# Norms before cross attention and before the router: rows transposed without gain and shift, which ScalarE adds on the transposed rows and GpSimd on the kept rows later

## The chip, the cores and the metric

One Trainium2 chip, one NeuronCore. The time is the device time of one execution in microseconds (us). Below, PE is TensorE, PEld its weight loads, DVE is VectorE, ACT is ScalarE, Pool is GpSimd and SP is SyncE, whose queue issues most of the transfers. Each engine works through its own instructions in the order of the program; semaphores tie the engines together.

## The reference

Eight sequences ("lanes" in the kernel) of 256 rows with 256 columns go through two layers. Cut to what matters:

```python
# layer 0: norm first
x = x + attn(ln(x, ln1), ln(x, ln1), causal=True)        # call 0
x = x + attn(ln(x, ln2), ctx, causal=False)              # call 1
x = x + ffn(ln(x, ln3))
# layer 1: norm after
x = ln(x + attn(x, x, causal=True), ln1_g, ln1_b)        # call 2; its norm is "stage 3"
x = ln(x + attn(x, ctx, causal=False), ln2_g, ln2_b)     # call 3; its norm is "stage FINAL"
x = ln(x + moe(x), ln3_g, ln3_b)                         # router: top 2 of 8 experts
# ln(x, g, b) = (x - mean) / sqrt(var + eps) * g + b ; attn has 16 heads of 16 columns
```

The two norms in question are the one that feeds call 3 (stage 3) and the one that feeds the router and the experts (stage FINAL). Both results are used twice: transposed, as the input of a projection, and as kept rows `x[lane]`, which go on as the residual (stage 3) or to the experts (FINAL). The inputs give every gain and shift values other than 1 and 0.

## The kernel before

There are 32 attention calls (4 calls of the model x 8 lanes), started one after the other in slots. A call lives for several slots: norm, transpose, q/k/v projections, a first pass of scores for the row maxima (`"max"`), a second pass of scores with the exponentials (`"head"`), weighing, output projection. Parts of neighbouring calls are interleaved on every engine. The order is written in a table: `STEPS` lists each step with a time (`AT[...]`, in units of which 16 make a slot), and each engine sorts its own steps by that time plus its entry in `LAG[engine]`. These numbers fix only an order in each queue; nothing else is done with them.

In `"head"`, PE writes the scores of a head into one of two PSUM buffers (`s_0`, `s_1`, line 766), and ACT turns them into `probs` (line 985). PE can't write the next head but one before ACT has read the buffer. So an ACT instruction that waits, or that stands ahead of an exponential, can stop PE.

The norm for a lane of stage 3, and of FINAL for lanes 0 to 6 (`by_three`), has four parts. DVE makes mean and variance (`norm`, steps "ln"). Pool makes `rstd` and `offset` (`inverse_root`, lines 561 to 568). ACT applies both to the kept rows in place (`scale`, line 896, two instructions). Pool multiplies by the gain and adds the shift (`gain_and_shift`, lines 575 and 577), and raises `gained`. PE (`rows_T` for stage 3, `final_T` for FINAL, both line 669) waits for `gained`, through `wait_norm`, and transposes the rows; ACT copies the transposed rows out of PSUM (lines 884 and 901). For FINAL the router's product (line 826), the choice of experts on DVE, `rank` on PE, and Pool's `scatter` (line 635, four indirect transfers a lane) follow, and SP stores the rows (`store`, line 521). Lane 7's FINAL norm is made on DVE alone (`apply_norm`: lines 1035 and 1040) after Pool's `rstd` (line 570), since nothing else is left to run beside it.

For the norms of layer 0 (stages 0, 1 and FFN) the transposed rows already get gain and shift on ACT (line 882), since there the kept rows don't need them.

Where PE has nothing left to interleave (lanes 5 to 7 of FINAL), the kernel has it transpose a constant (line 650, `s<-ident`). At the end of this part all engines meet, and the experts' part begins: its first instruction on the SP queue is the load of line 1316.

## Time and profile before

| | |
|---|---|
| median of 3 runs | 1204.1 us (1203.78 to 1204.68) |
| profiled execution: own time | 1205.83 us |
| its span, first to last instruction | 1204.1 us |
| PE busy | 1077.1 us, 89% |
| DVE, ACT, Pool busy | 846.2, 760.2, 518.6 us |
| mean granted TensorE clock | 0.957 |

The execution's own time is its span and 1.7 us around it; it is 0.14% above the median of the runs. In the granted clock, 1.00 is 2.4 GHz and 0.50 is 1.2 GHz. In the timeline a row gives start, duration, engine, line, operation and shapes, with xcount where like instructions are merged (the duration is then that of the whole group), and in brackets for how long the engine sat idle before it and what it waited for.

### The profile page before, as it was taken

The numbers are of one execution on the slowest core, as the hardware profiler recorded it, in microseconds if no ns is written. First come the engines' busy times: TensorE is split into PE (matmuls) and PEld (weight loads), VectorE is DVE, ScalarE is ACT, GpSimd is POOL, SyncE is SP. The second block draws the span as 40 slices with busy tenths as digits, with TensorE's granted clock in tenths as the row PEclk, the third lists the DMA queues.
The fourth block names the chain that finished last, engine by engine and source line by source line (L and its number), as shares of the span: only waits on it lengthen the run. The fifth ranks groups of instructions, "written<-read, shape, count | busy, mean of one in ns | idle before, by whom it ended". The sixth has DMA issues, their size and how long they took to land. (4 is left out here: it accounts for less than half of the span.)

```text
span 1204.1 us, 27676 instructions
## 1 busy us (share of the span) xinstructions
PE 1077.1 (89%) x9213; PEld 893.6 (74%) x9213; DVE 846.2 (70%) x2539; ACT 760.2 (63%) x1587; POOL 518.6 (43%) x736
## 2 busy tenths in 40 slices
PE   7788889999999999998899988878889999999960
PEld 6466666778888888876667666655679999999960
DVE  2677888777766666657777677763367988888846
ACT  4355565667666666645566666545258988898832
POOL 4345556322222223445566346532433454454544
PEclk9699999999999999999999999988889999999985
DMA  7584656654344433445566566622547787877764
GB/s 172 95 177 77 92 84 112 93 92 65 53 63 63 71 54 54 77 55 82 79 140 111 106 126 107 96 54 91 198 146 210 233 244 224 236 236 234 247 167 147
DMA packets 110892, 152.40 MB, mean 127 GB/s; under 512 B 23104, under 2 KB 95296, under 8 KB 104384
## 3 DMA queue, kind: packets, MB, share of 16 engines
q1 hardware_dynamic: 100560, 138.64, 51.8%
q0 software_dynamic: 8352, 10.80, 4.6%
q10 hardware_dynamic: 1872, 1.60, 1.1%
q8 instruction: 58, 0.95, 0.4%
q14 instruction: 50, 0.41, 0.2%
HBM read 78.39 MB, written 21.62 MB: 83 GB/s over the span
## 5 line engine op out<-in xcount | busy, mean ns | idle before, releaser
L985 ACT ACTIVATE probs<-s 128x384 f32<-128x384 f32 (+1 forms) x512 | 263.7, 541 | 130.3 <-PE s L766 117.1
L1069 DVE TENSOR_REDUCE neg_max<-s 128x2 f32<-128x512 f32 x256 | 167.9, 688 | 70.5 <-PE s L741 63.9
L766 PE MATMUL s<-q_stack,k_stack 98*128 98x256 bf16 (+1 forms) x1024 | 176.9, 263 | 16.4 <-ACT probs L985 14.0
L624 POOL TENSOR_SCALAR_AFFINE_SELECT probs<-probs 128x256 f32<-128x256 f32 x256 | 103.9, 417 | 176.6 <-ACT probs L985 172.6
L1066 DVE CUSTOM_DVE_ANT_0 s<-s,mask_qk 128x256 f32<-128x256 f32 x256 | 114.7, 448 | 66.2 <-PE s L738 58.4
L766 PEld LDWEIGHTS s<-q_stack,k_stack 98*128 98x128 bf16 x1024 | 87.9, 99 | 47.8 <-ACT probs L985 35.2
L785 PE MATMUL pv<-probs,v 128*32 128x256 f32 (+1 forms) x2048 | 116.0, 369 | 4.7 <-POOL probs L624 4.7
L741 PE MATMUL s<-k_stack,q_stack 96*128 96x256 bf16 x512 | 96.0, 276 | 13.3 <-DVE neg_max L1069 11.9
L1456 PE MATMUL moe<-rows_hi,e_w_hi 128*128 128x256 f32 x368 | 103.8, 282 | 2.6 <-DVE rows_lo L1574 2.6
L1456 PE MATMUL moe<-e_w_hi,e_hidden_hi 128*128 128x256 f32 x368 | 104.6, 284 | 0.0
L1456 PE MATMUL moe<-rows_hi,e_w_lo 128*128 128x256 f32 x368 | 103.2, 280 | 0.0
L1456 PE MATMUL moe<-rows_lo,e_w_hi 128*128 128x256 f32 x368 | 103.1, 280 | 0.0
L687 PE MATMUL work<-hT,w_qk 128*128 128x256 f32 x384 | 95.0, 392 | 8.8 <-ACTq L886 8.1
L1456 PE MATMUL moe<-e_w_lo,e_hidden_hi 128*128 128x256 f32 x368 | 102.9, 279 | 0.0
L1456 PE MATMUL moe<-e_w_hi,e_hidden_lo 128*128 128x256 f32 x368 | 102.7, 279 | 0.0
L1578 DVE TENSOR_TENSOR e_hidden_lo<-e_hidden,e_hidden_hi 128x512 fp32r<-128x512 f32 x92 | 77.0, 837 | 35.2 <-ACT e_hidden_hi L1538 27.8
L785 PEld LDWEIGHTS pv<-probs,v 128*32 128x32 f32 x2048 | 62.4, 113 | 46.5 <-issue 22.4
L1404 POOL DMA_INDIRECT x_rows<-result,token x46 | 80.0, 1738 | 25.2 <-issue 25.2
L737 PE MATMUL s<-k_stack,q_stack 96*128 96x256 bf16 x256 | 69.6, 283 | 21.2 <-DVE neg_max L1067 17.7
L687 PEld LDWEIGHTS work<-hT,w_qk 128*128 128x128 f32 x384 | 70.8, 194 | 20.3 <-ACTq L886 9.0
L1067 DVE CUSTOM_DVE_ANT_0 s<-s,mask_qk 128x128 f32<-128x128 f32 x256 | 84.9, 332 | 0.0
L1396 POOL TENSOR_TENSOR result<-result,share 128x512 f32<-128x512 f32 x23 | 30.6, 1329 | 118.7 <-issue 96.4
(207 smaller groups left out, 2895.0 us busy)
## 6 DMA issues: line engine op xcount, KB each, us to landing
w<-in_expert_w SPq DMA_DIRECT2D x26, 1024.0 KB, 5.3
k_stack<-k_part SPq DMA_DIRECT2D x192, 128.0 KB, 4.0
q_stack<-q_part SPq DMA_DIRECT2D x180, 128.0 KB
w_next<-in_expert_w SPq DMA_DIRECT2D x22, 1024.0 KB, 5.2
rows<-slots_x SPq DMA_DIRECT2D x25, 256.0 KB
slots_x<-filler SPq DMA_DIRECT2D x8, 518.0 KB
cT<-in_context SPq DMA_DIRECT2D x16, 256.0 KB, 5.9
e_b<-in_expert_b SPq DMA_DIRECT2D x24, 128.0 KB
```

Source lines behind the costliest of these rows:

```text
L624: pool.affine_select(out=blocks, in_=blocks, compare_op=ALU.is_ge, fill=0.0, base=0, pattern=[[0, TILES], [1, P]], channel_multiplier=-1). ...
L687: last = pe.matmul(dst[:, half * S:(half + 1) * S], w[:, k, half * P:(half + 1) * P], src[:, k, :], start=(k == 0), stop=(k == KC - 1))
L741: last = pe.matmul(dst[:, qt * S:(qt + 1) * S], q[:, qt * P:(qt + 1) * P], k, start=True, stop=True)
L766: last = pe.matmul(dst[:, kt * S:kt * S + S - q0], k[:, kt * P:(kt + 1) * P], q[:, q0:S], start=True, stop=True)
L785: last = pe.matmul(pv[32 * j:32 * j + 32, g * S + q0:(g + 1) * S], v[n % 3][:, (kt * H + hd) * VW:(kt * H + hd) * VW + 2 * DK], probs_of(n ...
L985: act.activation(probs_of(n, hd)[:, 0:width], s2[hd % 2][:, 0:width], ACT.Exp, scale=SCALE).then_inc(probs_ready, 1)
L1066: dve.tensor_tensor_reduce(src[:, 0:S], src[:, 0:S], mask_qk[:].rearrange("p b s -> p (b s)"), -1.0, -MASKED, ALU.add, ALU.min, neg_max[:, ...
L1067: dve.tensor_tensor_reduce(src[:, S:S + P], src[:, S:S + P], mask_qk[:, 1, :], -1.0, -MASKED, ALU.add, ALU.min, neg_max[:, 0, hd:hd + 1]). ...
L1069: dve.tensor_reduce(neg_max[:, :, hd], src[:].rearrange("p (t s) -> p t s", t=TILES), AX_X, ALU.max, negate=True).then_inc(s1_free, 1)
L1404: pool.indirect_dma_start(x_rows, bass.IndirectOffsetOnAxis(ap=token[i][:, m:m + 1], axis=0), result[i][:, m, :], None, compute_op=ALU.add ...
L1456: last = pe.matmul(dst, lhs[a], rhs[b], start=first and m == 0, stop=end and m == 2)
L1578: dve.tensor_tensor(hidden_lo[i][:, 2 * q:2 * q + 2, :], hidden[:, 2 * q:2 * q + 2, :], hidden_hi[i][:, 2 * q:2 * q + 2, :].bitcast(F32), ...
```

## The change

Stage 3: `rows_T` now waits only for ACT's `scale`; ACT multiplies by the gain and adds the shift while it copies the transposed rows (line 884 becomes the form of line 882). The kept rows get the gain in `add_bias` on Pool, after the transposes; the shift is added once to the output bias row, so that it comes with the bias.

FINAL: `final_T` waits only for `scale` (lanes 0 to 6) or DVE's apply (lane 7, now two instructions and not four). ACT's copy of line 901 becomes two instructions with gain and shift. Pool's `gain_and_shift` comes after the transposes, now for all eight lanes; `store` and `scatter` wait for it.

In the table ACT's "scale" goes later by 0.7, "final_T" earlier by 0.8, and "gain" from 59.3 to 62.5 (plus Pool's lag of 2.8, unchanged). "gain" is no longer a step of stage 3.

```diff
-LAG = {"scalar": {... "out": 1.4, "scale": 2.5, "halve": 0},
+LAG = {"scalar": {... "out": 1.4, "scale": 3.2, "halve": 0},
-      ... "final_ln": 59.3, "final_T": 64.8, "store": 63.1,
+      ... "final_ln": 59.3, "final_T": 64.0, "gain": 62.5, "store": 63.1,
...
-    return [(at, kind, lane, stage) for kind in (("ln", "scale", "gain") if by_three(lane, stage) else ("ln", "apply"))]
+    return [(at, kind, lane, stage) for kind in (("ln", "scale") if by_three(lane, stage) else ("ln", "apply"))]
...
         def wait_norm(engine, lane, stage):
             if by_three(lane, stage):
-                engine.wait_ge(gained, nth("gain", lane, stage))
+                engine.wait_ge(scaled, nth("scale", lane, stage))
...
             def store(lane, _):
-                wait_norm(sp, lane, FINAL)
+                sp.wait_ge(gained, nth("gain", lane, FINAL))
...
             def gain_and_shift(lane, stage):
-                pool.wait_ge(scaled, nth("scale", lane, stage))
+                pool.wait_ge(work_full, filled("final_T", lane, stage))
...
             def add_bias(lane, stage):
+                if lane == 0 and stage in POST:
+                    pool.tensor_tensor(bo[stage], bo[stage], shift[stage], ALU.add)
+                    pool.drain()
                 pool.wait_ge(work_full, filled("T", lane, stage))
+                if stage in POST:
+                    pool.tensor_tensor(x[lane], x[lane], gain[stage].unsqueeze(1).to_broadcast([P, TILES, D]), ALU.mult)
+                    pool.drain()
                 pool.tensor_tensor(x[lane], x[lane], bo[stage].unsqueeze(1).to_broadcast([P, TILES, D]), ALU.add).then_inc(x_biased, 1)
...
             def scatter(lane, stage):
+                pool.wait_ge(gained, nth("gain", lane, stage))
...
             def final_T(lane, stage):
                 act.wait_ge(work_full, filled("final_T", lane, stage))
-                act.activation(hT_of[FINAL][:].rearrange("p k s -> p (k s)"), bank("final_T", lane, stage)[:], ACT.Copy).then_inc(final_T_ready, 1)
+                for k in range(KC):
+                    last = act.activation(hT_of[FINAL][:, k, :], bank("final_T", lane, stage)[:, k * S:(k + 1) * S], ACT.Identity, bias=shift_column[stage][:, k:k + 1], scale=gain_column[stage][:, k:k + 1])
+                last.then_inc(final_T_ready, 1)
...
             def apply_norm(lane, stage):
-                if stage in POST:
-                    for i in range(TILES):
-                        dve.scalar_tensor_tensor(out=x[lane][:, i, :], in0=x[lane][:, i, :], scalar=mean_var[k][:, i, 0:1], in1=gain[stage], op0=ALU.subtract, op1=ALU.mult)
-                    dve.drain()
                 dve.wait_ge(rstd_ready, nth("ln", lane, stage))
```

How the queues change. On PE, around FINAL's transposes of lane 4 (`s_0` and `s_1` are the score buffers; line 741 is the pass for the maxima, line 766 the pass for the exponentials, 669 the transposes, 826 the router). Before:

```order
L766 MATMUL s_1<-q_stack,k_stack 128x256 x2
L741 MATMUL s_0<-k_stack,q_stack 128x256 x2
L741 MATMUL s_1<-k_stack,q_stack 128x256 x2
L766 MATMUL s_0<-q_stack,k_stack 128x256 x2
L741 MATMUL s_0<-k_stack,q_stack 128x256 x2
L766 MATMUL s_1<-q_stack,k_stack 128x256 x2
L669 MATMUL work<-ident,x 128x128 x4
L766 MATMUL s_0<-q_stack,k_stack 128x256 x2
L741 MATMUL s_1<-k_stack,q_stack 128x256 x2
L826 MATMUL work<-router_w,hT_ffn_final 128x8 x4
```

The same place after the change (the lines are 7 higher):

```order
L773 MATMUL s_1<-q_stack,k_stack 128x256 x2
L748 MATMUL s_0<-k_stack,q_stack 128x256 x2
L748 MATMUL s_1<-k_stack,q_stack 128x256 x2
L773 MATMUL s_0<-q_stack,k_stack 128x256 x2
L676 MATMUL work<-ident,x 128x128 x4
L748 MATMUL s_0<-k_stack,q_stack 128x256 x2
L773 MATMUL s_1<-q_stack,k_stack 128x256 x2
L773 MATMUL s_0<-q_stack,k_stack 128x256 x2
L748 MATMUL s_1<-k_stack,q_stack 128x256 x2
L833 MATMUL work<-router_w,hT_ffn_final 128x8 x4
```

The transposes stand one maximum pass and one head earlier. In lanes 0 to 3 they also move ahead of the q projection (line 687), which stands between those two.

On ACT, the same lane: the copy `u<-pv` of the weighed values, the norm's `scale` (`x<-x,offset_final`), the exponentials, and the copy of the transposed rows. Before:

```order
L949 ACTIVATE u<-pv 128x512
L896 ACTIVATE x<-x,offset_final,rstd_final 128x256 x2
L985 ACTIVATE probs<-s_0 128x512
L985 ACTIVATE probs<-s_1 128x512
L985 ACTIVATE probs<-s_0 128x512
L901 ACTIVATE hT_ffn_final<-work 128x512
```

After:

```order
L958 ACTIVATE u<-pv 128x512
L994 ACTIVATE probs<-s_0 128x512
L903 ACTIVATE x<-x,offset_final,rstd_final 128x256 x2
L994 ACTIVATE probs<-s_1 128x512
L994 ACTIVATE probs<-s_0 128x512
L909 ACTIVATE hT_ffn_final<-work,columns 128x256 x2
```

One exponential has moved ahead of `scale`, and two still stand between `scale` and the copy, which is now two instructions.

On Pool, the end of its queue in this part, after the change (lane 6's gain, shift and lane 5's scatter come first, then lane 7's `rstd`, gain and shift, and then the scatters of lanes 6 and 7 together):

```order
L575 TENSOR_TENSOR x<-x,row 128x2x256
L577 TENSOR_TENSOR x<-x,row 128x2x256
L642 DMA slots_x<-x,slot_of 33024x259 x4
L561 TENSOR_TENSOR var_eps_final<-mean_var_final,eps 128x2
L570 TENSOR_TENSOR rstd_final<-var_eps_final,minus_half 128x2
L575 TENSOR_TENSOR x<-x,row 128x2x256
L577 TENSOR_TENSOR x<-x,row 128x2x256
L642 DMA slots_x<-x,slot_of 33024x259 x8
```

Before, the fifth row was followed directly by the eight indirect transfers; the two operations of lines 575 and 577 are new there.

## Rows read from the trace of the kernel before

**Rows 1.** Page, part 2: granted TensorE clock in 40 equal slices, in tenths.

```profile
PEclk9699999999999999999999999988889999999985
```

**Rows 2.** Windows: start:end, length, busy us (count) of PE, PEld, DVE, ACT, POOL, clock.

```profile
713.00:739.00 26.00, 23.27 (x201) 16.78 (x200) 19.43 (x56) 16.94 (x37) 15.99 (x21) 1.00 0.60 103
786.57:812.57 26.00, 19.97 (x157) 12.51 (x156) 15.17 (x45) 11.72 (x25) 8.75 (x11) 0.77 0.10 33
```

**Rows 3.** Waits of PE from 687 to 792 (FINAL, lanes 0 to 3): total, times, longest.

```profile
PE s L766 <- ACT probs L985: 4.0, 9, 0.8
PE work L826 <- ACT hT_ffn_final L901: 1.2, 4, 0.3
```

**Rows 4.** Waits of PE from 786 to 870 (FINAL, lanes 4 to 7).

```profile
PE s L766 <- ACT probs L985: 6.7, 7, 2.1
PE work L669 <- POOL x L577: 3.7, 3, 1.3
```

**Rows 5.** Timeline of lane 4, PE, ACT and POOL.

```profile
792.48 1.09 ACT L896 ACTIVATE x<-x,offset_final,rstd_final 128x256 f32<-128x256 f32 x2 [0.47 <-POOL offset_final L568]
793.48 1.06 ACT L985 ACTIVATE probs<-s 128x512 f32<-128x512 f32 x2
...
794.11 0.61 PE L766 MATMUL s<-q_stack,k_stack 98*128 98x256 bf16 x2 [1.69 <-ACT probs L985]
...
796.61 1.11 PE L669 MATMUL work<-ident,x 128*128 128x128 f32 x4 [1.04 <-POOL x L577]
...
798.41 1.87 PE L826 MATMUL work<-router_w,hT_ffn_final 128*128 128x8 f32 x8
```

**Rows 6.** Timeline of lanes 5 and 6: scale and router of each.

```profile
821.43 1.09 ACT L896 ACTIVATE x<-x,offset_final,rstd_final 128x256 f32<-128x256 f32 x2 [0.48 <-POOL offset_final L568]
...
827.06 1.87 PE L826 MATMUL work<-router_w,hT_ffn_final 128*128 128x8 f32 x8
...
845.98 1.09 ACT L896 ACTIVATE x<-x,offset_final,rstd_final 128x256 f32<-128x256 f32 x2
...
851.59 1.87 PE L826 MATMUL work<-router_w,hT_ffn_final 128*128 128x8 f32 x8 [0.69 <-ACT hT_ffn_final L901]
```

**Rows 7.** Timeline of lane 2: FINAL's transposes.

```profile
745.31 0.60 PE L669 MATMUL work<-ident,x 128*128 128x128 f32 x4
```

**Rows 8.** Timeline in layer 0: DVE beside Pool, and ACT's copy with gain and shift.

```profile
260.66 0.74 DVE L1042 TENSOR_SCALAR h<-x,mean_var_main,rstd_main 128x256 f32<-128x256 f32 x2 [0.19 <-issue]
...
261.60 1.18 POOL L607 TENSOR_TENSOR x<-x,row 128x512 f32<-128x512 f32 x1
...
261.73 1.52 DVE L1042 TENSOR_SCALAR o<-x,mean_var_ffn,rstd_ffn 128x256 f32<-128x256 f32 x2 [0.34 <-POOL rstd_ffn L570]
...
264.01 1.02 ACT L882 ACTIVATE hT_ffn_final<-work,columns 128x256 f32<-128x256 f32 x2
```

**Rows 9.** Windows before the fall of the clock, and behind the routers of lanes 4, 5, 6.

```profile
790.00:794.00 4.00, 1.92 (x20) 0.99 (x12) 2.33 (x7) 2.85 (x7) 2.44 (x5) 1.00 0.02 4
798.40:804.30 5.90, 5.90 (x45) 3.52 (x44) 2.65 (x13) 1.68 (x3) 2.59 (x3) 0.50 0.26 91
827.10:835.00 7.90, 7.90 (x57) 5.00 (x57) 1.59 (x13) 2.75 (x5) 2.53 (x3) 0.50 0.19 67
851.60:858.90 7.30, 7.30 (x54) 5.09 (x55) 2.46 (x18) 1.30 (x3) 2.56 (x3) 0.50 0.22 75
```

**Rows 10.** Timeline of lane 7, the end of the attention part.

```profile
869.11 0.66 PE L669 MATMUL work<-ident,x 128*128 128x128 f32 x4 [0.69 <-DVE x L1040]
...
869.80 0.60 ACT L901 ACTIVATE hT_ffn_final<-work 128x512 f32<-128x512 f32 x1 [6.82 <-PE work L669]
...
872.41 0.96 POOL L635 DMA_INDIRECT slots_x<-x,slot_of  x1 [0.30 <-issue]
...
877.37 0.96 POOL L635 DMA_INDIRECT slots_x<-x,slot_of  x1 [3.99 <-DVE x L1156]
```

**Rows 11.** Timeline at stage 3, lane 0, between masked heads.

```profile
590.82 0.28 PE L737 MATMUL s<-k_stack,q_stack 96*128 96x256 bf16 x1 [1.20 <-DVE neg_max L1067]
```

More of the change, by code:

```diff
@@ L66 @@
 WARM_HEAD, WARM_TURN, WARM_OUT_T, WARM_WO, WARM_FINAL_T, WARM_ROUTER, WARM_RANK, WARM_EXPERTS = 2, 5, 11, 7, 34, 5, 12, 75
-LAG = {"scalar": {"T": 0.0, "q": 1.4, "k": 1.8, "v": 1.2, "out_T": 0, "up": 1.0, "head": 0.6, "shift": 0.8, "final_T": 0.5, "out": 1.4, "scale": 2.5, "halve": 0},
+LAG = {"scalar": {"T": 0.0, "q": 1.4, "k": 1.8, "v": 1.2, "out_T": 0, "up": 1.0, "head": 0.6, "shift": 0.8, "final_T": 0.5, "out": 1.4, "scale": 3.2, "halve": 0},
        "vector": {"max": 0.5, "q": 2.2, "k": 1.9, "shift": 2.8, "wo": 0.4, "down": 0.8, "turn": 0.7, "ln": 0, "apply": 3.1, "router": 0, "rank": 1.0, "pick": 0.8,
@@ L74 @@
       "bias": 13.1, "context": 8.9, "max": 14.8, "shift": 28.1, "head": 32.8, "weigh0": 43.7, "weigh1": 50.0, "turn": 52.5, "out_T": 55.1, "wo": 56.5,
-      "ffn_ln": 59.5, "ffn_T": 62.8, "ffn_bias": 67.4, "up": (65.5, 68.2, 72, 75), "down": (78.7, 83.2), "final_ln": 59.3, "final_T": 64.8, "store": 63.1,
+      "ffn_ln": 59.5, "ffn_T": 62.8, "ffn_bias": 67.4, "up": (65.5, 68.2, 72, 75), "down": (78.7, 83.2), "final_ln": 59.3, "final_T": 64.0, "gain": 62.5, "store": 63.1,
       "router": 65.5, "rank": 67.8, "scatter": 85.5, "post_ln": -15.1}
@@ L124, in plan_call @@
         later = AT["later"] * (B - 1 - lane)
-        steps += [(AT[kind] + later, kind, lane, FINAL) for kind in ("final_T", "router", "pick", "rank", "place", "scatter")]
+        steps += [(AT[kind] + later, kind, lane, FINAL) for kind in ("final_T", "gain", "router", "pick", "rank", "place", "scatter")]
         steps += [(at + later, "share", lane, i) for i, at in enumerate(AT["shares"])]
@@ L223, in attention_part @@
         w_vo = ring(2, "w_vo", [P, 2, KC, D])
-        columns = sb("columns", [P, 3 * CALLS * KC + FC + 2 * len(PRE) * KC])
+        columns = sb("columns", [P, 3 * CALLS * KC + FC + 2 * len(PRE + POST) * KC])
         row = sb("row", [P, (3 + 2 * len(POST)) * D + E])
@@ L234, in attention_part @@
         b1 = of_columns(FC)
-        pre_gain, pre_shift = ({k: of_columns(KC) for k in PRE} for _ in range(2))
+        gain_column, shift_column = ({k: of_columns(KC) for k in PRE + POST} for _ in range(2))
         def of_row(i):
@@ L880, in rows_T @@
                     dst, src = (hT_of[FFN] if stage == FFN else hT[CALL[stage, lane] % 2])[:, k, :], bank("T", lane, stage)[:, k * S:(k + 1) * S]
-                    if stage in PRE:
-                        last = act.activation(dst, src, ACT.Identity, bias=pre_shift[stage][:, k:k + 1], scale=pre_gain[stage][:, k:k + 1])
+                    if stage in PRE + POST:
+                        last = act.activation(dst, src, ACT.Identity, bias=shift_column[stage][:, k:k + 1], scale=gain_column[stage][:, k:k + 1])
                     else:
@@ L1032, in apply_norm @@
                     h_read[0] = filled("T", lane, stage)
-                if stage in POST:
-                    for i in range(TILES):
-                        dve.scalar_tensor_tensor(out=x[lane][:, i, :], in0=x[lane][:, i, :], scalar=mean_var[k][:, i, 0:1], in1=gain[stage], op0=ALU.subtract, op1=ALU.mult)
-                    dve.drain()
                 dve.wait_ge(rstd_ready, nth("ln", lane, stage))
                 for i in range(TILES):
-                    if stage in POST:
-                        last = dve.scalar_tensor_tensor(out=x[lane][:, i, :], in0=x[lane][:, i, :], scalar=rstd[k][:, i:i + 1], in1=shift[stage], op0=ALU.mult, op1=ALU.add)
-                    else:
-                        last = dve.tensor_scalar((h_of[FFN] if stage == FFN else h)[:, i, :], x[lane][:, i, :], mean_var[k][:, i, 0:1], rstd[k][:, i:i + 1], ALU.subtract, ALU.mult)
+                    dst = x[lane] if stage in POST else h_of[FFN] if stage == FFN else h
+                    last = dve.tensor_scalar(dst[:, i, :], x[lane][:, i, :], mean_var[k][:, i, 0:1], rstd[k][:, i:i + 1], ALU.subtract, ALU.mult)
                 last.then_inc(h_ready, 1)
@@ L1697, in packed @@
                                     + [column(a[b.format("v")]) for _, b in ATTENTION] + [column(a["L0_xattn_ffn_b1"])]
-                                    + [column(a[n + "_g"]) for n in PRE_NORMS] + [column(a[n + "_b"]) for n in PRE_NORMS], axis=1)
+                                    + [column(a[n + "_g"]) for n in PRE_NORMS + POST_NORMS] + [column(a[n + "_b"]) for n in PRE_NORMS + POST_NORMS], axis=1)
     out["row"] = np.concatenate([a[b.format("o")] for _, b in ATTENTION[0:2]] + [a["L0_xattn_ffn_b2"]] + [a[n + "_g"] for n in POST_NORMS] + [a[n + "_b"] for n in POST_NORMS]
```

## The prediction

> **What bounds the kernel now.** I read the page's slices first. PE is busy for 89% of the span, so a gain has to come out of PE's idle time or out of its clock, and the row of clocks shows where both are poor in the attention part: slices 27 to 30 (783 to 903 us) stand at 8, where the slices before them stand at 9 (9 stands for anything from 0.9 up) [rows 1]. These are the last lanes of call 3 and the start of the experts' part. The windows say what that means: in 26 us around lane 1's FINAL norm PE is busy for 23.27 us at a granted clock of 1.00, and in 26 us around lane 4's for 19.97 us at 0.77, with DVE and ACT far from full in both [rows 2]. So the early lanes are short of about 2.7 us of PE a slot, and lanes 4 to 6 suffer from idle PE and a slow PE together.
>
> Next I asked PE for its waits. In lanes 0 to 3 it waits 4.0 us for exponentials and 1.2 us (four times 0.3) for ACT's copy of the transposed rows ahead of the router [rows 3]. In lanes 4 to 7 it waits 6.7 us for exponentials and 3.7 us (three times, lanes 4 to 6) for Pool's shift [rows 4]. The timeline of lane 4 shows the mechanism. ACT idles 0.47 us with `scale` at the head of its queue, because Pool's offset isn't there, spends 1.09 us in it, and only then makes the exponentials that free the score buffers; PE stands for 1.69 us. Then PE reaches the transposes and stands 1.04 us more, until Pool has finished gain and shift, which begin after `scale`. The router starts at 798.41 [rows 5].
>
> The clock falls right there. In the 4 us from 790 PE is busy for 1.92 us at clock 1.00; from the router on, for 5.9 us, it is 0.50, that is 1.2 GHz, and PE is busy without a pause; so it is behind the routers of lanes 5 and 6, for 7.9 and 7.3 us [rows 9]. While PE is fully busy at 0.50, up to half of the time is a loss.
>
> **The change part by part.**
>
> *Lanes 4 to 6, the router's start.* In the new order an exponential goes ahead of `scale`, into the 0.47 us in which ACT idled. In lane 4 `scale` still ends at 792.48 + 1.09 = 793.57. The transposes may start then, and take 0.60 us at full clock [rows 7] or 1.11 at half [rows 5]. ACT's copy stands behind two exponentials, 1.06 us [rows 5], and takes 1.02 us in its new form, whose row exists in layer 0 [rows 8]: the router starts at 793.57 + 1.06 + 1.02 = 795.7, hidden or not by the transposes at either clock (793.6 + 1.11 + 1.02 gives 795.8). That is 2.7 us earlier than 798.41. Lane 5 by the same sum: 821.43 + 1.09 + 1.06 + 1.02 = 824.6 against 827.06, 2.4 us. In lane 6 ACT didn't idle ahead of `scale` [rows 6], so the exponential put ahead costs its own 0.53: 845.98 + 0.53 + 3.17 = 849.7 against 851.59, 1.9 us. Together 7.0 us, all on PE, which behind the router is busy without a pause [rows 9]. The least that this can be is the Pool wait alone, 3.7 us [rows 4], less the dearer copies; the most is all of both waits, 10.4 us. I take 7.0.
>
> *Lanes 0 to 3.* Here the transposes didn't wait for Pool (no such wait in this stretch). Gained are the four waits on exponentials that stand behind `scale`, of which the longest is 0.8 [rows 3]; one more is like it and two are about half as long, some 2.5 of the 4.0 us. Gained too are the router's 1.2 us, since the copy now comes a q projection ahead of it. Lost: the transposes now stand right behind a head, and `scale` an exponential later (0.53), and the copies for stage 3 and FINAL cost ACT about 0.4 us more each (1.02 for 0.60 [rows 8, 10]). I set a new wait of the transposes on `scale` at 0.3 us a lane, 1.2 in all. Sum: 3.7 - 1.2 = 2.5 us; the bounds are 0 (the new wait as long as the old) and 5.2 (all waits of rows 3).
>
> *Stage 3 in the masked calls.* Pool loses gain and shift there and gets one of them back in `add_bias`; ACT's `scale` moves behind `u` and an exponential. But PE's wait in this place is on DVE's row maximum, 1.20 us, not on ACT [rows 11], and DVE's queue doesn't change. I put it at 0; the fewer Pool operations between the masks might give 0.5 us, and the slower copies (0.4 us of ACT a lane, behind work of its own) might take that.
>
> *Moved work on Pool and SP.* In lanes 0 to 6 gain and shift now end some 1 to 2 us later, with the q/k splits, `inverse_root` and `scatter` of other lanes behind them on Pool and the stacking transfers behind `store` on SP. Their users come much later: the maxima pass of the new call starts more than half a slot on. Cost 0; if that cover were gone it would be about 1 us a lane.
>
> *The end.* Lane 7's transposes start as before (its two last DVE instructions stay, in a form that took 0.74 us a pair elsewhere [rows 8]); they end at 869.77 [rows 10]. Two things follow. ACT's copy takes 0.42 us more, which delays the router, the shares and lane 7's scatter, 877.37, by as much. And Pool's gain and shift (2 x 1.18 us, as for the same shape in [rows 8], and a gap) now stand ahead of both scatters: from 869.9 to 872.4, then lane 6's four transfers, which start 1.27 us apart (0.96 and an issue gap of 0.30 [rows 10]), 5.2 us in all, so lane 7's first at 877.8. Either way about +0.5 us on the start of the experts' part. There is a second price. In layer 0 a pair of DVE instructions took 0.74 us alone and 1.52 us beside a Pool operation of 1.18 us [rows 8]. If DVE's small instructions are held like that while Pool does lane 7's gain and shift, the end costs up to 1.0 us more. I take +0.6.
>
> The Trainium skill's page "GPSIMD Engine Reference" (section "1. Specifications") says that GpSimd shares its SBUF interface with VectorE's instructions in a two-port mode or with two SBUF inputs; a rule against this change, which puts Pool beside DVE's last chain. By it the end would cost 1.6 us, not 0.6; the trace agrees that such a price exists, and its own bound is the one used above.
>
> *The clock.* The 5.9, 7.9 and 7.3 us at half speed behind the routers [rows 9] would give back half at full speed: 3.0, 4.0 and 3.6, together 10.6 us. The pauses that precede the fall shrink: in lane 4 from 1.69 + 1.04 = 2.7 us [rows 5] to about 0.3 (one exponential) and 0.5 (the transposes on `scale`), 0.8 us. The two later lanes keep about 2 us each, since there PE has no maxima pass to fill them. I expect that one of the three falls doesn't come, 3.5 us, of which I count 2.4, since at full clock the exponentials (0.53 us a head) become the next limit.
>
> *Sum.* -7.0 - 2.5 + 0.6 - 2.4 = -11.3 us on the profiled execution's 1205.8 us: 1194.5. The median of the runs is 1.7 us below that execution: **1192.8, say 1193 us**, 0.9% faster. A difference below 0.2%, 2.4 us, can't be told from none here.
>
> **The rivals.**
>
> *The clock stays at 1.00 in all three lanes.* For it: the pauses shrink in each. Against it: some 2 us of waits remain in 5 us in lanes 5 and 6. It gives -8.9 and the whole 10.6 less a third for ACT, -16: 1188 us, and down to 1185. The Trainium skill's page "TensorE: Matmul & The Clock Gate" (section "Part 1: The HAM clock gate") says that recent activity of the array releases the throttle and that the chip's looking at it is free-running, so that the point of the switch moves from run to run. By that rule all three may stay high in one execution and none in the next, and the runs would scatter by a few us where they now agree within 0.9.
>
> *The waits come back elsewhere.* PE's new wait for `scale` takes what the earlier exponentials gave, in lanes 0 to 3 wholly, and in lanes 4 to 6 only Pool's 3.7 us is saved, less 1.2 us of dearer copies. With 0.6 at the end: -2, and with half of my sum in the late lanes -5: 1199 to 1202. For it: `scale` is itself later by one exponential. Against it: in lane 4 and 5 that exponential falls into ACT's idle time [rows 5, 6].
>
> *Nothing to measure.* The slots are bound by something that these rows don't show, such as DVE at 19.43 of 26 us [rows 2]: within 2.4 us of 1204.
>
> *Slower.* New pauses of PE ahead of the transposes in lanes 0 to 3 make the clock fall there too, where it is 1.00 now. A fall like those of rows 9, about 8 us, costs 4 us while PE is as busy as there. Four falls cost 16 us and give 1204 + 16 - 9 = 1211. It decides from the third on, at a new wait of well over the 0.3 us assumed. Against it: the waits removed there are as long as those added.
>
> **How the numbers follow.** My forecast, 1190 to 1197 by itself: 0.64. Clock high in all three lanes: 0.12. Waits that come back: 0.12, of which a little ends within 0.2%. Nothing to measure: 0.07. Slower: 0.05. Faster by over 0.2%: 0.64 + 0.12 + 0.11, so 0.87; within 0.2%: 0.08; slower: 0.05. The range for 8 in 10 goes from 1186 (most of the first rival) to 1200 (the better half of the second).
>
> **What would show it.** Right: no wait of PE's L676 on Pool; `scale` behind an exponential; the router's start 2 to 3 us after `scale` in lanes 4 to 6; lanes 0 to 3 about 0.6 us shorter a slot; lane 7's scatter about 8 us after the end of its transposes. For the clock: fewer windows at 0.50 between 780 and 860. Wrong would be: PE's L676 waiting over 1 us on ACT's L903, PE's wait on exponentials still at 6 to 7 us in the late lanes, a clock below 1.00 before lane 4, or a tail longer by over 1 us.

## The result, and the profile after

The changed kernel takes 1209.9 us (median of 19 runs, 1205.0 to 1217.2) against 1204.1 us for the kernel before (19 runs, 1201.1 to 1210.9). The ratio is 1.0039, 95% interval 1.0026 to 1.0053: 0.4% slower, where 0.9% faster was forecast. The profiled execution took 1210.0 us, its span is 1208.1 us. The record doesn't name the chip of these runs. As the experiments show, the number depends on it: on two other chips programs with the same change are 0.5 to 0.9% faster than before.

First the page of the changed kernel, part 2, granted clock in 40 slices, to be laid beside [rows 1]:

```profile
PEclk9699999999999999999999999988999999999985
```

Slices 29 and 30 rose from 8 to 9, so the clock did improve. Then the waits of PE in the changed kernel, first over lanes 0 to 3 of FINAL (against [rows 3]):

```profile
PE work L833 <- DVEq L1058: 3.0, 4, 0.8
PE work L676 <- ACT x L903: 1.3, 4, 0.3
PE s L773 <- ACT probs L994: 1.0, 4, 0.2
```

and over lanes 4 to 7, from 786 to 875 (against [rows 4]):

```profile
PE s L773 <- ACT probs L994: 2.4, 6, 0.6
PE work L676 <- ACT x L903: 2.3, 3, 1.0
PE work L805 <- issue: 2.1, 1, 2.1
PE work L833 <- ACT hT_ffn_final L909: 2.1, 4, 0.8
```

The waits for exponentials fell from 4.0 to 1.0 and from 6.7 to 2.4 us, the wait on Pool is gone, and the transposes' new wait on `scale` is 0.3 us a lane in lanes 0 to 3, all as forecast. In lanes 4 to 6 that wait is longer, 2.3 us for the three. Two things are new. The router (L833) waits 0.8 us a lane for L1058, DVE's release of a work bank. And once PE waits 2.1 us for "issue", that is for nothing that the profile shows.

The closing stretch of the changed kernel shows more of the latter. PE's last transposes (75 of the identity, `WARM_EXPERTS`, ahead of the experts' part) and Pool's transfers, from the timeline:

```profile
873.43 5.55 PE L657 MATMUL s<-ident 128*128 128x128 f32 x49
879.63 0.27 PE L657 MATMUL s<-ident 128*128 128x128 f32 x1 [0.66 <-issue]
880.36 0.27 PE L657 MATMUL s<-ident 128*128 128x128 f32 x1 [0.45 <-issue]
881.06 0.32 PE L657 MATMUL s<-ident 128*128 128x128 f32 x1 [0.44 <-issue]
882.49 0.27 PE L657 MATMUL s<-ident 128*128 128x128 f32 x1 [1.10 <-issue]
883.90 4.23 PE L657 MATMUL s<-ident 128*128 128x128 f32 x22 [1.15 <-issue]
...
872.40 1.04 POOL L642 DMA_INDIRECT slots_x<-x,slot_of  x1 [0.17 <-issue]
...
881.36 0.96 POOL L642 DMA_INDIRECT slots_x<-x,slot_of  x1 [0.30 <-issue]
888.39 0.53 POOL L1410 MEMSET result<- 128x512 f32 x1 [6.07 <-POOLq L208]
```

The last scatter is issued at 881.4, but the experts' part begins at 888.39, when PE has finished: behind the first 49 its instructions came one at a time, some 0.7 or 1.4 us apart (I call this a crawl), and the last 22 then ran mostly at half clock. The kernel before did its 75 in 8.4 us, ended them at 881.6, and began the experts' part at 884.33.

The start of each lane's router says where time went. Differences to before, in us:

| profile | lane 0 | lane 3 | lane 4 | lane 5 | lane 6 | lane 7 | experts' part | span |
|---|---|---|---|---|---|---|---|---|
| before, start | 695.09 | 772.97 | 798.41 | 827.06 | 851.59 | 870.46 | 884.33 | 1204.1 |
| changed | +3.03 | +4.87 | +3.15 | +2.12 | +0.04 | +0.21 | +4.06 | +4.0 |
| e5 (before's order, wide columns) | +2.48 | +2.49 | +2.50 | +3.42 | +2.16 | +1.67 | +1.75 | +4.5 |
| e9 (changed, tiles 256 bytes on) | +0.68 | +1.29 | -1.66 | -6.74 | -9.28 | -11.99 | -11.95 | -12.1 |
| e16 (changed kernel again, on chip D) | +3.50 | +3.18 | +0.77 | -2.35 | -4.91 | -7.63 | -7.59 | -4.9 |
| e17 (changed kernel, third time, on the chip of e5) | +3.54 | +6.52 | +4.73 | +0.53 | -1.68 | -0.30 | +3.81 | +5.3 |
| e18 (as e9, on the chip of e5) | +0.31 | +0.85 | -0.64 | -3.60 | -5.74 | -4.40 | -0.01 | -0.6 |

The changed kernel (second row) is late by 3 us when FINAL begins, loses 1.8 us in lanes 0 to 3, gains 4.8 us in lanes 4 to 6, and loses 3.9 us in the closing stretch. From the start of the experts' part to the end it takes 319.7 us, as before does (319.8); over all profiles of this case that stretch varies from 317 to 323 us, which is to be kept in mind where single spans are compared.

### The profile page after: what moved, and what is told of

The parts are those of the page before. It is cut to its first block and busy times, and to the rows that moved or that the text cites. A ratio compares the mean times of both kernels' runs of the same rounds, so it can differ in the third digit from the quotient of the medians.

```text
span 1208.1 us, 27677 instructions
## 1 busy us (share of the span) xinstructions
PE 1074.4 (89%) x9213; PEld 889.1 (74%) x9213; DVE 843.3 (70%) x2537; ACT 764.0 (63%) x1595; POOL 512.7 (42%) x731
## 5 line engine op out<-in xcount | busy, mean ns | idle before, releaser
L1538 ACT ACTIVATE e_hidden<-moe,e_b 128x256 f32<-128x256 f32 x184 | 75.7, 462 | 8.9 <-PE moe L1459 8.9
```

Of the source, the lines that this page charges most:

```text
L1538: last = act.activation(hidden[:, f, :], up_bank[q][:, m * GROUP:(m + 1) * GROUP], ACT.Gelu, bias=b1_e[i][:, f:f + 1])
```

## The experiments

There were eighteen runs in five groups. The kernels of a group ran on one chip, beside the kernel before on the same chip; e5 to e8 and e17, e18 ran on the same chip, B, and the groups on C and D came between them. Ratios are to the kernel before.

| run | what it is | chip | median us | ratio, 95% interval |
|---|---|---|---|---|
| e1 | change at stage 3 alone | A | 1211.9 | 1.0052 (1.0031 to 1.0073) |
| e2 | change at FINAL alone | A | 1207.1 | 1.0007 (0.9993 to 1.0021) |
| e3 | FINAL, lanes 4 to 6 alone | A | 1203.5 | 0.9982 (0.9965 to 1.0000) |
| e4 | changed, 40 closing transposes | A | 1205.3 | 1.0002 (0.9986 to 1.0018) |
| e5 | before, 8 unread columns more | B | 1209.6 | 1.0044 (1.0027 to 1.0061) |
| e6 | changed, lane 7's gain behind lane 6's scatter | B | 1205.9 | 1.0025 (1.0011 to 1.0038) |
| e7 | FINAL, lanes 0 to 6 | B | 1203.3 | 1.0004 (0.9990 to 1.0019) |
| e8 | as e3, new columns loaded apart | B | 1201.8 | 0.9979 (0.9963 to 0.9995) |
| e9 | changed, tiles 256 bytes on | C | 1193.4 | 0.9913 (0.9900 to 0.9925) |
| e10 | e6 with tiles 256 bytes on | C | 1195.6 | 0.9926 (0.9903 to 0.9950) |
| e11 | e3 with tiles 256 bytes on | C | 1193.1 | 0.9909 (0.9892 to 0.9926) |
| e12 | e7 with tiles 256 bytes on | C | 1195.7 | 0.9925 (0.9912 to 0.9937) |
| e13 | changed, only the stacks put back | D | 1195.4 | 0.9923 (0.9900 to 0.9946) |
| e14 | changed, all but the stacks put back | D | 1197.8 | 0.9939 (0.9916 to 0.9962) |
| e15 | e9, split parts aligned too | D | 1196.4 | 0.9933 (0.9910 to 0.9955) |
| e16 | changed kernel again | D | 1199.8 | 0.9952 (0.9931 to 0.9974) |
| e17 | changed kernel, third time | B | 1211.0 | 1.0044 (1.0025 to 1.0063) |
| e18 | e9 again | B | 1206.9 | 1.0011 (0.9992 to 1.0030) |

The kernel before took 1206.0 us on A, 1203.9 and 1204.1 on B, 1203.7 on C and 1203.8 on D.

**First group: which part of the change loses?** My theory: the loss arises around FINAL and in the closing stretch; the rival: stage 3. One condition picks the norms that are changed (e1: `stage != FINAL`; e2: `stage == FINAL`; e3: `stage == FINAL and 4 <= lane < 7`), all other norms keep the code and the queue times of before:

```diff
+def turned(lane, stage):
+    return stage in POST and (stage == FINAL and 4 <= lane < 7)
```

> The change is made for the norm of stage 3 alone; FINAL's norm keeps the order of before in all lanes. Theory A (the loss arises in call 3 around FINAL and in the closing stretch): time as before within 0.2%, 1202 to 1207 us. Theory B (the dearer two-instruction copies and Pool's moved gain cost something in every masked call of stage 3 and the wider columns load costs 1 to 2 us at the start): slower than before by 2 to 5 us, and then it carries most of the change's loss.

> The change is made for FINAL's norm alone, in all lanes; stage 3 is as before. Theory A: it carries the whole loss, +3 to +6 us against before: lanes 0 to 3 longer by some 3 us together (the router waits for its work bank, which the k projection holds), lanes 4 to 6 shorter by some 7 us, the closing stretch longer by some 4 us, and the wider columns load the rest. Theory B: faster than or equal to before, since stage 3 carries the loss.

> The change is made for FINAL's norm of lanes 4 to 6 alone; lanes 0 to 3, lane 7 and stage 3 are as before. Theory A: the gain of 7 us in lanes 4 to 6 stays without the early cost and without the dearer closing stretch: 1194 to 1200 us, 0.4 to 0.8% faster than before. Rival: what lanes 4 to 6 gain is given back at the end whoever causes it (the closing stretch is set by something else than lane 7's own form): within 0.2% of before.

e4 is the changed kernel with fewer closing transposes:

```diff
-... WARM_RANK, WARM_EXPERTS = 2, 5, 11, 7, 34, 5, 12, 75
+... WARM_RANK, WARM_EXPERTS = 2, 5, 11, 7, 34, 5, 12, 40
```

> The changed kernel with 40 transposes of the identity instead of 75 ahead of the experts' part on PE. If PE's filler transposes set the start of the experts' part, as the one profile of the changed kernel shows (PE at them until 888.1 us, the last scatter issued at 881.4 us), it starts some 3 us earlier and the time falls by 2 to 4 us against the changed kernel, to 1206 to 1208 us. If that profile shows a rare event or the fillers buy clock for what follows, the time stays at 1209 to 1211 us or rises.

e1 was the slowest of all, 0.5%, though nothing in it touches FINAL: theory A missed. e2, with the part that should lose, lost nothing that can be told. e3 gained 0.2%, less than the 7 us. e4 gained a little more than expected (1205.3 us for 1206 to 1208): its experts' part starts at 884.0, and PE ends its transposes at 877.1. What all four, and the changed kernel, have in common and before has not is the wider tile `columns`. In all of them the first exponential comes 2.0 to 2.7 us later than before, and around 200 us PE waits for a transfer; the changed kernel's row of waits there, which before has not:

```profile
PE s L748 <- DMA q_stack<-q_part: 0.7, 1, 0.7
```

**Second group: the wide columns, and the eight scatters in a row.** e5 is the kernel before, with eight columns more that nothing reads. e6 moves one step of Pool in the changed kernel:

```diff
+        if lane == B - 1:
+            steps = [(AT["scatter"] - SLOT - 2.7 if kind == "gain" and arg == FINAL else at, kind, lane, arg) for at, kind, lane, arg in steps]
```

e7 is `turned` with `stage == FINAL and lane < 7`. e8 is e3 with the first load as narrow as before:

```diff
-            act.dma_start(columns[:], t["columns"]).then_inc(loaded_columns, 16)
+            act.dma_start(columns[:, 0:first_columns], t["columns"][:, 0:first_columns]).then_inc(loaded_columns, 16)
...
+                    sp.dma_start(columns[:, first_columns:], t["columns"][:, first_columns:]).then_inc(loaded_columns, 16)
```

> The kernel before, in its own order, with nothing of the change but the eight further columns in the first load (52 instead of 44 values a partition), which nothing reads. Theory A (the load is part of the loss): the first exponential comes some 2 us later, as in all five profiles with the wide load, and the time is 1 to 3 us above before (+0.1 to +0.25%). Theory B (that one profile of before had an early start by chance): within 0.1% of before.

> The changed kernel, all 75 closing transposes on PE, but Pool does lane 7's gain and shift behind lane 6's four scatters instead of ahead of them, so that the eight scatters of lanes 6 and 7 don't stand in one row. If PE's closing transposes crawl because of eight scatters without a pause, the crawl (single transposes 0.7 us apart) is gone and the experts' part starts 3 to 4 us earlier: 1205 to 1207 us, as with 40 transposes. If the crawl comes from the number of transposes, or by chance, the time stays at 1208 to 1211 us.

> FINAL's norm changed in lanes 0 to 6, lane 7 and stage 3 as before. It stands between the run with lanes 4 to 6 alone (1203.5) and the one with all lanes (1207.1). If lanes 0 to 3 cost by the router's wait for its bank, it is 1 to 3 us slower than lanes 4 to 6 alone, 1204 to 1206 us; the closing stretch is as short as before, since lane 6's and lane 7's scatters have their pause again. If lane 7's form has no part in the loss, it is at 1206 to 1208 us.

> As the run with FINAL's norm changed in lanes 4 to 6 alone, but the first load of columns is as narrow as before (44 values a partition) and the eight others come by a load of their own much later. If the wide load costs 1 to 2.5 us, this one gives 1201 to 1202.5 us, 0.3 to 0.4% faster than before. If it doesn't, it repeats that run: 1203 to 1204 us.

e5 is 0.44% slower than before, more than I gave it, with not one instruction of the change in it. Of its 4.5 us in the profile, 2.2 stand already at the first exponential (53.59 us for 51.36), 2.5 at the routers of lanes 0 to 4, and 1.75 at the start of the experts' part; the rest arises behind it, in the stretch that varies by itself. e8 repeats e3 (on another chip), so it isn't the load. What is left is the tile itself: eight values more move every tile behind `columns` by 32 bytes. In the kernel before, the stacks of q and k, which SP's stacking transfers write, begin at a multiple of 256 bytes of a partition (q's at 96000 = 375 x 256); in all the others so far 32 bytes past one (96032). The DMA view from 100 to 700 us (queue, packets, MB, share of 16 engines; then the issues, with median us to landing), before:

```profile
q1 hardware_dynamic: 48367, 48.19, 50.9%
...
k_stack<-k_part SPq DMA_DIRECT2D x145, 128.0 KB, 4.0
cT<-in_context SPq DMA_DIRECT2D x14, 256.0 KB, 5.8
```

and e5:

```profile
q1 hardware_dynamic: 48214, 48.05, 58.4%
...
k_stack<-k_part SPq DMA_DIRECT2D x147, 128.0 KB, 4.4
...
cT<-in_context SPq DMA_DIRECT2D x14, 256.0 KB, 6.9
```

The same bytes take the engines 15% longer. In the trace's packets the median one of 1024 bytes takes 138 ns in e5 and 139 in the changed kernel, against 111 before. The Trainium skill, page "DMA: Bandwidth & Descriptors", section "How a descriptor splits into AXI transactions", says that a descriptor is cut into transactions of at most 256 bytes, each of which must begin at a multiple of 256, so that one that starts off a multiple can need one more. By that rule 1024 bytes take five instead of four, a quarter more, an estimate; the trace agrees with 138 and 139 for 111. Counted in the page's beats of 32 bytes it would be 33 instead of 32, an estimate too, and that is not what the trace shows. The page speaks of the bytes that are read, though; which side counts here, the fourth group shows.

e6 shows no crawl in its closing transposes (all 75 in 8.38 us) and is 0.2% better than the changed kernel on its chip (e17, 1.0044), though the intervals overlap. e7 with lane 7 as before lies 0.4% under e17.

**Third group: everything 256 bytes on.** In each kernel `columns` gets 56 unused values, so that later tiles shift by 256 bytes instead of 32 (and the load gets its 52 values by number):

```diff
-        columns = sb("columns", [P, 3 * CALLS * KC + FC + 2 * len(PRE + POST) * KC])
+        columns = sb("columns", [P, 3 * CALLS * KC + FC + 2 * len(PRE + POST) * KC + 56])
...
-            act.dma_start(columns[:], t["columns"]).then_inc(loaded_columns, 16)
+            act.dma_start(columns[:, 0:52], t["columns"]).then_inc(loaded_columns, 16)
```

> The changed kernel with 56 unused values behind its 52 columns, so that every later tile stands 256 bytes, not 32 bytes, behind its place in the kernel before. Theory A (the 32 bytes slow the stacking transfers): the median packet of 1024 bytes between 100 and 700 us takes 111 ns as before, not 139; PE no longer waits for a stacked q near 200 us; the loss of 4 to 5 us that the kernel before showed with the eight further columns alone is gone: 1203 to 1206 us, with the crawl of PE's closing transposes left. Rival (the wide columns cost by their load or by something else than the place of the tiles): packets stay near 139 ns or the time stays at 1208 to 1211 us.

> The changed kernel with the tiles 256 bytes on and with lane 7's gain and shift behind lane 6's scatters. If the losses add up (4.5 us by the place of the tiles, 2 to 4 us by the crawl), this gives 1199 to 1203 us, 0.1 to 0.4% faster than before. If the place of the tiles has no part, 1205 to 1207 us.

> FINAL's norm changed in lanes 4 to 6 alone, with the tiles 256 bytes on. With the tiles 32 bytes on it gave 0.18% less than before. If the place costs 0.4% in every kernel, this is 0.5 to 0.65% faster than before, 1196 to 1199 us: the gain of 7 us that the prediction worked out for these lanes, undisturbed. If not, it repeats 0.2%.

> FINAL's norm changed in lanes 0 to 6, lane 7 and stage 3 as before, with the tiles 256 bytes on. Against the run with lanes 4 to 6 alone in the same places it shows what lanes 0 to 3 give: by the prediction's sum 2.5 us less, by the router's new wait 1 to 3 us more. I expect 1 to 2 us more, 1197 to 1201 us.

All four are 0.7 to 0.9% faster than before, far better than expected. e9, the change in full, takes 1193.4 us: the forecast was 1193. Its clocks and its closing stretch:

```profile
PEclk9689999999999999999999999998989999999985
```

```profile
861.23 8.38 PE L657 MATMUL s<-ident 128*128 128x128 f32 x75
...
860.20 1.04 POOL L642 DMA_INDIRECT slots_x<-x,slot_of  x1 [0.17 <-issue]
...
869.15 0.96 POOL L642 DMA_INDIRECT slots_x<-x,slot_of  x1 [0.30 <-issue]
872.38 0.53 POOL L1410 MEMSET result<- 128x512 f32 x1 [2.27 <-POOLq L208]
```

There is no crawl, with the same eight scatters in a row. So the place of the tiles seemed to cost 16 us here and 5 in e5, which asked for a test of the place by itself.

**Fourth group: which tiles?** e13 has unused bytes around the stacks only, e14 is its opposite, e15 moves the split parts, which the stacking transfers read, to a multiple of 256 as well, and e16 is the changed kernel unaltered. The edit of e13:

```diff
+        sb("pad_front", [P, 56])
         q_stack = ring(3, "q_stack", [P, H, S], BF16)
         k_stack = ring(3, "k_stack", [P, H, S], BF16)
+        sb("pad_back", [P, 8])
```

> The changed kernel with only the six tiles of the stacked q and k (and nothing else) put back on their old places against multiples of 256 bytes, by 224 unused bytes ahead of them and 32 behind. Theory A (the writes into the stacks are what got slower): packets of 1024 bytes back at 111 to 113 ns, PE's hidden stalls gone, 1192 to 1196 us. Theory B (another tile, such as the split parts that these transfers read, the rows of x that the scatters read, or the contexts): it stays at 1205 to 1211 us.

> The opposite: all tiles on their old places against multiples of 256 bytes but the stacked q and k, which stand 32 bytes on. Theory A: as slow as the changed kernel, 1206 to 1211 us, packets at 139 ns. Theory B: 1192 to 1196 us, packets at 111 ns.

> The changed kernel with the tiles 256 bytes on, and the split parts of q and k, which the stacking transfers read, moved from 64 bytes past a multiple of 256 to a multiple. If a source off the multiple costs as a destination does, the packets of 1024 bytes fall below 111 ns and the time by 1 to 4 us against 1193.4; if only the destination counts, it stays at 1193 to 1194 us.

> The changed kernel once more, beside the three others on the same chip: 1207 to 1212 us, packets of 1024 bytes at 139 ns. If PE's crawls belong to the slow stacking transfers and not to one execution, this profile has again single closing transposes 0.7 us apart and dependents of PE that start over 1 us after PE's recorded end; if they were chance, it has none and the time is near 1206 us.

The share of queue q1 from 100 to 700 us, in this order: e13, e14, e15, e16.

```profile
q1 hardware_dynamic: 48191, 48.03, 51.5%
```

```profile
q1 hardware_dynamic: 47930, 47.79, 58.3%
```

```profile
q1 hardware_dynamic: 48201, 48.03, 51.7%
```

```profile
q1 hardware_dynamic: 47876, 47.73, 58.7%
```

That settles the tiles: with the stacks alone on the multiple the transfers are as quick as before (51.5%), with the stacks alone off it they are as slow as in the changed kernel (58.3%). Moving the source to a multiple changes nothing (51.7% at 1196.4 us): with the stacks on the multiple the median packet of 1024 bytes takes 113 ns where the split parts begin 96 or 64 bytes past one (e13, e9), and 115 where they begin on one (e15). So it is the side that is written that counts; for the side that is read, of which the page speaks, no cost shows. The loads of `cT`, in packets of 2048 bytes, say the same: 105 to 108 ns where `cT` begins on a multiple (before, e9, e14, e15), 114 where it begins 32 bytes past one (e5, e13, e16), a smaller step (over all profiles 105 to 111 against 111 to 116). In time the medians go the same way, 1195.4 (e13), 1197.8 (e14), 1199.8 (e16), but with intervals that overlap, so no more can be read from this chip than a size of 0.3 to 0.4% (e13 against e16). e14 lies between them: that the stacks alone cost all of that time isn't shown.

The surprise is e16: the changed kernel, which had been 0.4% slower than before, is here 0.5% faster, and its closing transposes don't crawl:

```profile
865.59 8.39 PE L657 MATMUL s<-ident 128*128 128x128 f32 x75
```

So neither the crawl nor most of the 16 us comes from the place of the tiles: the changed kernel of the first result and e16 have the same places. The theory behind the third group fell in part.

**Fifth group: changed and e9 side by side.**

> The changed kernel a third time, on whichever chip it falls. Its first runs gave 1209.9 us (+0.39%), its second, on another chip, 1199.8 us (-0.48%), with the kernel before at 1204 us in both. If what differs belongs to the chip, this falls near one of the two, 1207 to 1212 with late dependents of PE in its profile, or 1197 to 1202 without any. If it is spread from run to run, it lies between them with a wide spread.

> The changed kernel with the tiles 256 bytes on, again, beside the former on one chip. The place of the tiles by itself should give 0.3 to 0.4% (e13 against e16 on one chip), so 1193 to 1196 us on a chip as the last two. If the chip disturbs, this tells whether the 256 bytes shield from it (1193 to 1196 us still) or not (1203 to 1207 us).

They fell on chip B, that of e5 to e8, and the first result came back: +0.44% for the changed kernel, and +0.11% for the very program that was 0.87% faster than before on chip C. e18's closing stretch:

```profile
874.95 0.32 PE L657 MATMUL s<-ident 128*128 128x128 f32 x1 [0.45 <-issue]
876.37 0.27 PE L657 MATMUL s<-ident 128*128 128x128 f32 x1 [1.10 <-issue]
877.08 0.27 PE L657 MATMUL s<-ident 128*128 128x128 f32 x1 [0.44 <-issue]
877.81 0.46 PE L657 MATMUL s<-ident 128*128 128x128 f32 x1 [0.46 <-issue]
879.21 4.85 PE L657 MATMUL s<-ident 128*128 128x128 f32 x22 [0.94 <-issue]
```

The crawl belongs to the chip, then, not to the place of the tiles. Its forerunners stand further up in the same profiles. In e2 (chip A; its line numbers differ from the changed kernel's) the transposes of `o` end by the profile at 787.4, but ACT's copy, which waits for nothing else, starts 1.4 us later, right behind four scatters (782.8 to 787.7):

```profile
786.78 0.60 PE L694 MATMUL work<-ident,o 128*128 128x128 f32 x4
788.75 0.84 ACT L985 ACTIVATE oT<-work,columns 128x256 f32<-128x256 f32 x2 [3.75 <-PE work L694]
```

I looked in every trace, from 690 to 880 us, for instructions of ACT and DVE that stood idle until a wait for PE ended, over 0.8 us after the end that the profile gives for that work of PE. The changed kernel's first profile and all those of chips A and B but one have between two and seven, of 0.9 to 2.9 us, e1, e3 and e8 too; each starts while Pool issues its scatters or at most 1.1 us behind the last. The eight profiles of chips C and D have none. The exception on B is e5, the one with the order of before, whose longest is 0.75 us; before's own profile has 0.74.

The table says how much hangs on it. At lane 0's router, 695 us into the kernel, e17 and e16 (the changed kernel on B and on D) are within 0.1 us of each other, and e18 and e9 (the aligned one on B and on C) within 0.4. At the start of the experts' part they are 11.4 and 11.9 us apart, of which 4.1 us arise between the routers of lanes 6 and 7, in both pairs, and 4.1 to 4.4 in the closing stretch. From there to the end neither pair differs by more than 1.2 us, though Pool issues indirect transfers there too. So in these profiles the chip costs time only behind lane 0's router, in the stretch in which Pool scatters the lanes' rows. It isn't more traffic: over 11 us with the last scatters in them the DMA engines carry 656 packets, 1.32 MB, in the changed kernel's first profile and in e16 alike. Nor is it the hour, as far as this can tell: B was used ahead of C and D and behind them, and its profiles with the change are late both times.

## Why the prediction was wrong

The forecast was 1193, range 1186 to 1200; the result is 1209.9. The same program, but with its tiles 256 bytes on, gave 1193.4 on chip C. That this meets the forecast is in part luck, since two misses of 3 to 4 us cancel in it (lanes 0 to 3, and the clock). The sum failed in three places: the term for lanes 0 to 3, -2.5 us, measured nil; the end left out PE's closing transposes, which cost 3.9 us in the changed kernel; and it had no term for the place of the tiles, 4 to 6 us. PE's late instructions around the scatters, which no row of before shows, make the rest. The steps:

**Lanes 4 to 6, the router's start: right.** It was to be 3.2 us behind the start of `scale` in each; it is 3.0 us in all three lanes of e9, and in those of the changed kernel's first profile. Lane 6 of e9:

```profile
839.28 1.09 ACT L903 ACTIVATE x<-x,offset_final,rstd_final 128x256 f32<-128x256 f32 x2
...
842.31 1.06 PE L833 MATMUL work<-router_w,hT_ffn_final 128*128 128x8 f32 x8 [0.79 <-ACT hT_ffn_final L909]
```

From lane 3's router to lane 6's, e9 gains 1.29 + 9.28 = 10.6 us, of which the sum had 7.0 and 2.4 for the clock. Single profiles differ here: in the others of the full change on chips C and D the three lanes give 7.8 to 10.6, and 4.8 in the changed kernel's own.

**The clock: right in kind, too small.** One of the three falls was not to come. It was the third: behind lane 6's router the clock is 1.00 in e9 (and was in the changed kernel), where [rows 9] show 0.50; behind lane 5's it is still low. Windows of e9:

```profile
796.70:802.00 5.30, 4.91 (x61) 3.25 (x62) 3.98 (x16) 2.90 (x6) 4.38 (x5) 1.00 0.29 100
820.20:828.00 7.80, 7.68 (x58) 4.82 (x59) 1.70 (x13) 2.95 (x7) 5.39 (x6) 0.56 0.30 104
842.20:849.50 7.30, 6.55 (x75) 5.23 (x76) 4.14 (x25) 1.35 (x4) 5.38 (x6) 1.00 0.40 138
```

In e9 there is no fall right behind lane 4's router either (in e16 there is). Lane 6 to lane 7 gives 2.7 us more, in e16 too, where that stretch also runs at full clock. So, if the waits gave their 7.0, the clock gave back some 6 us in e9 (10.6 + 2.7 - 7.0), not 2.4. That split is a sum, not a measurement. In the changed kernel's own profile the clock is 1.00 there as well, and the 2.7 us are missing all the same: ACT's copy of the weighed values starts at 856.85, 2.3 us behind PE's recorded end, in the middle of four scatters:

```profile
856.85 0.60 ACT L958 ACTIVATE u<-pv 128x512 f32<-128x512 f32 x1 [4.57 <-remote]
```

**Lanes 0 to 3, -2.5: failed.** Waits of exponentials and of the router's copy went as forecast, 4.0 to 1.0 and 1.2 to 0, and the new wait on `scale` is the 0.3 assumed. What the step did not see is the router's bank. Its work bank is the one that the next k projection filled, and DVE's `k_rest` frees it after ACT's `k_part`, ahead of which the dearer copy of the transposed rows now stands, in two instructions: 3.0 us of waits at L833, the same in e9. Lane 1 before, where `k_part` comes first:

```profile
717.85 0.83 ACT L912 ACTIVATE k_part<-work,columns 128x256 bf16<-128x256 f32 x2
...
720.02 0.59 ACT L901 ACTIVATE hT_ffn_final<-work 128x512 f32<-128x512 f32 x1
```

and in e9:

```profile
718.28 1.03 ACT L909 ACTIVATE hT_ffn_final<-work,columns 128x256 f32<-128x256 f32 x2
719.48 0.84 ACT L921 ACTIVATE k_part<-work,columns 128x256 bf16<-128x256 f32 x2 [0.17 <-issue]
...
720.35 0.88 DVE L1055 SCALAR_TENSOR_TENSOR k_rest<-work,columns,k_part 128x256 f32<-128x256 f32 x2 [0.29 <-ACT k_part L921]
...
721.50 1.03 PE L833 MATMUL work<-router_w,hT_ffn_final 128*128 128x8 f32 x8 [0.76 <-DVEq L1058]
```

From lane 0's router to lane 3's e9 loses 0.6 us and e10 gains 0.3: the gain is nil, not 2.5. The rival "the waits come back elsewhere" was right here, and wrong in lanes 4 to 6. The kernels that change lanes 0 to 6 (e7, e12) are no faster than those that leave lanes 0 to 3 alone on the same chip (e8, e11).

**Stage 3, 0: no sign against it.** e1, stage 3 alone, is at 1.0052, and e5, which has only its wide columns, at 1.0044, on another chip and with intervals that overlap. On chip C lane 0's router stands at +0.7 and +0.3 with stage 3 changed (e9, e10) and at +1.0 and +1.4 without (e11, e12).

**Moved work on Pool and SP, 0: no sign against it** in e9.

**The end, +0.6: right by itself, wrong on chips that crawl.** From lane 7's router to the experts' part before takes 13.87 us and e9 13.91; e11 and e12, which leave lane 7 as it was, take 13.29 and 13.17 on the same chip as e9, 0.6 to 0.7 less. Of the further 1.0 us for DVE beside Pool there is no sign. In the changed kernel it takes 17.72, in e18 18.26. The sum took Pool and ACT for the only ones that can be late, and left out PE's closing transposes, which ended 2.7 us before the experts' part began and so had little room. With 40 instead of 75 (e4) or with a pause between the scatters (e6) the kernel is 0.4 and 0.2% better than e17; e4's size rests on two chips.

**The missing term: the place of the tiles.** No step priced `columns` growing from 44 to 52 values. It costs 0.3 to 0.4%, 4 to 6 us by the medians: 0.44% in e5 against before, 0.33% in e17 against e18, 0.29% in e16 against e13, each pair on one chip. That the transfers are slower, and by which tiles, is shown; the time rests on three pairs that agree, of which only the first is clear of the overlap of the intervals.

**The chip.** The rest, 0.9 to 1.0% (e17 against e16, e18 against e9), goes with the chip, for the same programs, while the kernel before keeps to 1204 on B, C and D. It goes together with PE's late and crawling instructions near Pool's scatters. Together: -0.9% of the change, +0.35% of the place, +0.95% of the chip give +0.4%. The prediction had no term for either of the last two. The forecast's rival "slower" expected falls of the clock in lanes 0 to 3. One came; window of the changed kernel:

```profile
699.70:703.10 3.40, 3.40 (x33) 1.39 (x26) 2.30 (x11) 0.54 (x1) 1.77 (x2) 0.50 1.07 138
```

Half of 3.4 us is at most 1.7 us, so it isn't the cause.

What stays open: why PE's instructions are late on A and B and not on C and D, and why before's order hardly suffers from it. That the eight scatters in a row bring on the crawl is supported (on the chips where PE is late, all four profiles with eight scatters and 75 transposes crawl there, behind the 49th or 50th, namely the first, e2, e17 and e18, and none of the six with a pause between the two fours does), but eight in a row do no harm on C and D. Whether the late instructions are the whole of the chip's cost isn't shown either: it arises in the same stretch, and in single profiles.

## What to carry to other kernels

A change that grows one tile moves all that are allocated behind it. Before a new order is judged, see whether the tiles that DMAs write stand as before against multiples of 256 bytes; a few unused bytes put them back, and the share of the DMA queue over a long window shows it at once. Run the old kernel with nothing but the new sizes: e5 was worth more than the three runs that took the change apart. And a difference of half a per cent that was measured on one chip should be measured on another before it is explained: here the sign changed.

The version to keep is e9 or e11, 0.9% faster than before on chip C; e11 changes three lanes only, and with the tiles 32 bytes on, on chips A and B (e3, e8), it was 0.2% faster where the full change was slower. With aligned tiles it wasn't run on A or B.

## What was not expected of the hardware

A DMA that writes rows of 1024 bytes to SBUF takes 138 to 141 ns a packet (median) instead of 111 to 115 when the tile begins 32 bytes past a multiple of 256; the place of the tile that it reads (96 or 64 bytes past, or none) makes no difference. Packets of 2048 bytes, loaded from HBM, take 111 to 116 ns instead of 105 to 111.

On two of four chips PE's instructions come late while GpSimd issues indirect DMAs one behind another: a dependent engine starts 0.9 to 2.9 us behind PE's recorded end, and behind eight in a row single instructions of PE come 0.7 or 1.4 us apart. One profile there, of the order of before, shows none of it. The changed programs on the two other chips show none either, and the same program is 0.9 to 1.0% faster there.
